# Second layer of a graph network kernel: node rows kept as two halves in F32R, one 320-column product per node tile, and one tile of each edge group fetched by TensorE

## The reference

```python
h = jnp.maximum(_layernorm(x, axis=-1), 0.0)
ss, vv = (s[src], v[src])                      # rows of h by source node
dot = jnp.einsum('eui,ei->eu', vv, e1)
out0 = C0 * (ss * e0 @ W1 + dot * INV3 @ W2)
...                                            # out1: three more products of ss, vv, e0, e1
m_agg = jax.ops.segment_sum(m, dst, num_segments=n)
...                                            # hs, hv = m_agg @ Ws, Wv
return x + jax.nn.relu(h)
```

## Time and profile before

| what | value |
|---|---|
| runs | 1919.09, 1921.43, 1923.35 us |
| profiled execution, span (the page gives no other time of it) | 1922.0 us |
| PE busy | 1773.5 us, 92% |
| POOL busy | 1405.2 us, 73% |
| DVE busy | 1376.6 us, 72% |
| ACT busy | 179.3 us, 9% |
| second layer, first to last gather | 1023.07 to 1904.05 us |

### The profile page before, as it was taken

The page is one execution under the profiler, slowest core; times in us unless marked ns, Lnnn a source line. Parts: engine busy times, 40 slices in busy tenths (PEclk is TensorE's granted clock), DMA queues, the critical chain, the costliest instruction groups (busy, mean ns, idle before and its releaser), DMA issues.

```text
span 1922.0 us, 59005 instructions
## 1 busy us (share of the span) xinstructions
PE 1773.5 (92%) x16922; PEld 1554.1 (81%) x16922; DVE 1376.6 (72%) x2841; ACT 179.3 (9%) x415; POOL 1405.2 (73%) x1498
## 2 busy tenths in 40 slices
PE   8989898989999988889875999999999999999998
PEld 6567676767667676767645899999999999999998
DVE  7888887878787878878878466656656565666654
ACT  5100000010010100000032000000000000000000
POOL 4677777777777777777755777777777777777774
PEclk9999999999999999999987999999999999999999
DMA  7433344333343333333323323223222323223323
GB/s 251 122 103 106 104 105 106 105 105 106 95 114 94 105 105 104 106 105 105 103 77 97 76 73 78 76 72 77 73 76 73 76 72 76 76 73 76 75 74 92
DMA packets 113339, 181.97 MB, mean 95 GB/s; under 512 B 31272, under 2 KB 80720, under 8 KB 112848
## 3 DMA queue, kind: packets, MB, share of 16 engines
q0 software_dynamic: 70272, 120.03, 25.2%
q1 hardware_dynamic: 35592, 55.14, 9.1%
q10 hardware_dynamic: 7112, 2.94, 0.6%
HBM read 170.94 MB, written 7.05 MB: 93 GB/s over the span
## 4 chain that ended last, share of the span: by engine, by line
POOL 43%; PE 26%; issue 18%; ACTq 6%; DVE 4%; DMA 1%; ACT 1%; POOLq 0%; DVEq 0%
POOL g L841 42%; PE sums L1147 8%; PE sums L1132 5%; PE w_ps L1100 5%; ACTq L733 5%; PE hid_ps L1086 3%; PE sums L1157 2%; DVE work L997 1%; ACT work L867 1%; DMA g<-node_table 1%; ACTq L730 1%; DVE work L991 1%; PE w_ps L604 1%; PE sums L576 0%; ACT lin_sb L873 0%
## 5 line engine op out<-in xcount | busy, mean ns | idle before, releaser
L841 POOL DMA_INDIRECT g<-node_table,src x1453 | 1379.4, 949 | 468.4 <-issue 439.1
L1147 PE MATMUL w_ps<-H,work 128*128 128x160 f32 x2900 | 404.3, 299 | 1.5 <-issue 1.5
L1147 PEld LDWEIGHTS w_ps<-H,work 128*128 128x128 f32 x2900 | 398.0, 190 | 1.7 <-issue 1.7
L997 DVE TENSOR_TENSOR work<-w_ps,g 128x384 f32<-128x384 f32 (+3 forms) x693 | 297.4, 456 | 54.0 <-PE w_ps L1100 33.0
L1016 DVE STREAM_TRANSPOSE turned<-sums 128x160 f32<-128x160 f32 x232 | 79.5, 342 | 322.6 <-PE sums L1157 224.5
L1100 PE MATMUL w_ps<-fc_sb,work 64*128 64x224 f32 x1612 | 219.1, 378 | 96.3 <-ACT work L867 59.4
L1132 PEld LDWEIGHTS sums<-work,sel 128*32 128x32 f32 x6448 | 198.5, 111 | 111.1 <-issue 68.2
L1100 PEld LDWEIGHTS w_ps<-fc_sb,work 64*128 64x128 f32 x1612 | 169.5, 191 | 130.6 <-DVE work L991 82.6
L945 DVE TENSOR_TENSOR sel<-mixed,sh 128x896 f32<-128x896 f32 x232 | 251.6, 1084 | 27.6 <-DVE mixed L941 2.1
L1132 PE MATMUL sums<-work,sel 128*32 128x160 f32 x6448 | 246.9, 304 | 1.9 <-DVE work L991 1.0
L1136 PE MATMUL sums<-g,sel 128*128 128x160 f32 x1612 | 238.2, 301 | 9.8 <-DMA g<-node_table,src 9.8
(11 more groups left out here) (103 smaller groups left out, 709.5 us busy)
## 6 DMA issues: line engine op xcount, KB each, us to landing
g<-node_table SPq DMA_DIRECT2D x2304, 0.6 KB
g<-node_table ACTq DMA_DIRECT2D x2304, 0.6 KB
feat<-edge_feat_dram SPq DMA_DIRECT2D x60, 512.0 KB
g<-node_table,src POOLq DMA_INDIRECT x1453
named<-src_rows_dram SPq DMA_DIRECT2D x30, 192.0 KB
X<-x_dram SPq DMA_DIRECT2D x5, 400.0 KB, 6.6
named<-src_rows_dram SPq DMA_DIRECT2D x30, 64.0 KB
sh<-edge_sh_dram SPq DMA_DIRECT2D x1, 1624.0 KB, 9.0
```

What stands on the lines that cost most here:

```text
L841: nc.gpsimd.indirect_dma_start(out=g[:, slot(p, u, j), :], out_offset=None, in_=table[layer], in_offset=bass.IndirectOffsetOnAxis(ap=src[: ...
L997: nc.vector.tensor_tensor(blocks(at), w[:, :, 2 * S_CH + j * V_CH:2 * S_CH + (j + 1) * V_CH].unsqueeze(2).to_broadcast([P, n, m, V_CH]), r ...
L1147: last = nc.tensor.matmul(found_at[:, i, 0:D], match[layer][i][:, t, :], H[:, t, :], start=(t == 0), stop=(t == NT - 1))
```

## The change

Only the second layer and what lies before it change (beside a regrouping of the first layer's code that leaves its instructions as they were).

- `split` holds for each node tile 320 columns in F32R: the upper half (ACT copies `H` with its conversion) and the remainder (VectorE subtracts that from `H`). One `find` is now 25 products of F32R operands with 320 columns.
- TensorE fetches one tile of every group (`PICKS`: tile 6 of groups 0, 1, 2 of a turn, tile 5 of group 3), 115 in all, and GpSimd issues no gather for these.
- ACT casts the indices for a whole turn in two pieces: `cast_early` for three tiles into PSUM (`hid_ps`), `cast_late` for the fourth into SBUF (`late_named`). VectorE's casts go.
- VectorE adds the two 160-column halves from PSUM into `g` (`join`, a TENSOR_REDUCE over two) in the place of ACT's copy.
- VectorE's order in a stage is now select, turn, compare for the group after the next, join for the next group. Match tiles: groups 1 and 3 of a turn share one; one lies over `H`, so the layer's compares wait until the table's DMAs have read `H`.

```diff
-PICKED = ((2,), (0, 2))
-MORE_AT = ((), (0,1,2))
+PICKS = ((0, 6), (1, 6), (2, 6), (3, 5))
+MATCH_OF = (0, 1, 2, 1)
+BANK_OF = (0, 1, 2, 3)
...
+        split = nc.alloc_sbuf_tensor_at("split", [P, NT, 2 * D], F32R, offset=arena_at)
+        match = [nc.alloc_sbuf_tensor_at(f"match{b}", [P, NT, P], F32R, offset=at)
+                 for b, at in enumerate((arena_at + 4 * SPLIT, arena_at + 4 * (SPLIT + NPAD), H_at))]
...
+        early_named = hid_ps[:, 0:EARLY * P].rearrange("p (i e) -> p i e", e=P)
+        late_named = arena_part(SPLIT + 2 * NPAD, P)
+        wanted_of = [early_named[:, i, :] for i in range(EARLY)] + [late_named]
...
+                        others |= {j for v, j in PICKS if v == u}
...
+                def cast_early(f, nxt):
+                    act.wait_ge(named_in[layer], 16 * f + (16 * nxt + 16))
+                    if nxt:
+                        act.wait_ge(match_done, NP * f + EARLY)
+                    nc.scalar.activation(early_named, named[:, 0:EARLY, :], ACT.Copy).then_inc(named_cast, 1)
+                def cast_late(f, nxt):
+                    if nxt:
+                        act.wait_ge(match_done, NP * f + NP)
+                    nc.scalar.activation(late_named, named[:, EARLY, :], ACT.Copy).then_inc(late_cast, 1)
...
+                def compare(f, i, nxt, s):
...
+                    dve.wait_ge(named_cast if i < EARLY else late_cast, f + (nxt + 1))
+...
                    nc.vector.tensor_tensor(match[MATCH_OF[i]][:], wanted_of[i].unsqueeze(1).to_broadcast(wide),
+                                            node_id_sb[:].unsqueeze(2).to_broadcast(wide),
+                                            ALU.is_equal).then_inc(match_done, 1)
+                def join(f, p, i, nxt, s):
+                    dve.wait_ge(found, NP * f + (NP * nxt + i + 1))
+                    nc.vector.tensor_reduce(g[:, slot(p, u, j), :], banks[:, BANK_OF[i], 0:2 * D].rearrange("p (h c) -> p c h", h=2),
+                                            AXX, ALU.add).then_inc(found_copied, 1)
...
-                        last = nc.tensor.matmul(found_at[:, i, 0:D], match[layer][i][:, t, :], H[:, t, :],
+                        last = nc.tensor.matmul(banks[:, BANK_OF[i], 0:2 * D], match[MATCH_OF[i]][:, t, :], split[:, t, :],
...
+            act.wait_ge(h1_ready, BY_ACT)
+            nc.scalar.activation(split[:, 0:BY_ACT, 0:D], H[:, 0:BY_ACT, :], ACT.Copy).then_inc(upper_ready, 1)
+            act.wait_ge(h1_by_dve, len(by_dve))
+            nc.scalar.activation(split[:, BY_ACT:, 0:D], H[:, BY_ACT:, :], ACT.Copy).then_inc(upper_ready, 1)
...
+            for h, at in enumerate((slice(0, BY_ACT), slice(BY_ACT, NT))):
+                dve.wait_ge(upper_ready, h + 1)
+                last = nc.vector.tensor_tensor(split[:, at, D:2 * D], H[:, at, :], split[:, at, 0:D].bitcast(F32), ALU.subtract)
...
+            dve.wait_ge(rows1_out, 16 * len(pieces))
```

More of the change, by code:

```diff
@@ L28 @@
 I32 = mybir.dt.int32
+F32R = mybir.dt.float32r
 ALU = mybir.AluOpType
@@ L640, in edge_layer, with picks_at, exists, fetched @@
             pass_of = {}
[L641 to L658, removed]
-                u, nxt = (o + ahead) % UNROLL, (o + ahead) // UNROLL
[L661 to L670, removed]
+            def picks_at(o, s, ahead):
+                u, nxt = (o + ahead) % UNROLL, (o + ahead) // UNROLL
+                if s is not None and s + ahead >= GROUPS:
+                    return []
+                return [(i, nxt) for i in range(NP) if PICKS[i][0] == u]
+            def exists(i, s):
+                return s is None or s < GROUPS and PICKS[i][1] < tiles_of(s)
+            def fetched(s):
+                return s is None or UNROLL <= s < GROUPS - UNROLL
+            found_at = sums[:, 0, 256:256 + D]
             def tiles_of(s):
@@ L834, in gather @@
                     p = (it - LEAD) % PERIOD if it >= LEAD else -1
[L835 to L844, removed]
+                    group = UNROLL * it + u
+                    n = tiles_of(group)
+                    others = {TILES - 1} if by_row_at(p, u, TILES - 1) else set()
+                    if own_weights:
+                        others |= {TILES - 1} if u == PICKED0 and fetched(group) else set()
+                    else:
+                        others |= {j for v, j in PICKS if v == u}
+                    for h, (a, b) in enumerate(CHUNKS):
+                        own = [j for j in range(max(a, skip), min(b, n)) if j not in others]
+                        for j in own:
+                            missing = b - max(a, skip) - len(own) if j == own[-1] else 0
+                            nc.gpsimd.indirect_dma_start(
+                                out=g[:, slot(p, u, j), :], out_offset=None, in_=table[layer],
+                                in_offset=bass.IndirectOffsetOnAxis(ap=src[:, TILES * group + j:TILES * group + j + 1], axis=0),
+                            ).then_inc(gathered[u][h], 16 + 16 * missing)
                 with passes(pool) as r:
@@ L948, in select, with match_rows @@
                                             ALU.mult).then_inc(sel_done, 1)
[L950 to L961, removed]
+                def match_rows(f):
+                    dve.wait_ge(named_in[layer], 16 * f + 32)
+                    dve.wait_ge(match_done, f + 1)
+                    nc.vector.tensor_copy(wanted, named[:, 0, :]).then_inc(named_read, 1)
+                    dve.wait_ge(named_read, f + 2)
+                    dve.wait_ge(found, f + 1)
@@ L1039, in stage @@
                         else:
-                            compare(f, p, e, PICKED[layer][0], 0, 0, True)
-                    if s is None or s < GROUPS:
-                        select(f, it, o, s)
-                        if pick_after(o, s, p, 2):
-                            compare(f, p, e, (o + 2) % UNROLL, *pick_after(o, s, p, 2), s is not None and s + 2 < UNROLL)
+                            for u in range(2):
+                                for i, nxt in picks_at(0, s, u):
+                                    compare(f, i, nxt, s + u)
+                    live = s is None or s < GROUPS
+                    before = None if s is None else s - 1
+                    if live:
+                        select(f, it, o, s)
+                    if not own_weights:
+                        if s is None or 1 <= s <= GROUPS:
+                            turn(f, o - 1, before)
+                        if s == 0:
+                            for i, nxt in picks_at(o, s, 0):
+                                join(f, p, i, nxt, s)
+                        for i, nxt in picks_at(o, s, 2) if live else []:
+                            compare(f, i, nxt, None if s is None else s + 2)
+                        for i, nxt in picks_at(o, s, 1) if live else []:
+                            join(f, p, i, nxt, None if s is None else s + 1)
+                    if live:
                         if s == GROUPS - 2:
@@ L1056, in stage @@
                                 else:
-                                    compare(f, p, e, 2, 0, 1, False)
-                    if s is None or 1 <= s <= GROUPS:
-                        turn(f, o - 1, None if s is None else s - 1)
+                                    match_rows(f)
+                    if own_weights and (s is None or 1 <= s <= GROUPS):
+                        turn(f, o - 1, before)
                     if s == GROUPS:
```

142 lines of the change are left out of this document (98 added, 44 removed).

## The result

The changed kernel takes 1955.4 us (median of 4 runs, 1953.0 to 1957.7) and the kernel before 1920.3 beside it: a ratio of 1.018 with an interval of 1.0166 to 1.0193, so 1.8% slower. The prediction said 1956 us. The profiled execution has a span of 1955.8 us.

The account below looks back on a forecast made before the run. GpSimd's back-to-back gathers were taken as the bound, TensorE within 1% of it: span 1922.0 - 37.6 (30 gathers) + 70 (28 holds) + 2 (between layers) = 1956.4, so 1956 us; own range 1942 to 1982, taken as 1925 to 1984.

Parts of the forecast that it names:

- TensorE's part: Second layer's finds: 0.139 us a product, 3.5 us a find, PE busy 69.9 us a period in place of 90.8.
- GpSimd as the clock: Second layer: GpSimd's gathers run back to back at 1.2538 us a step and stay the bound, 95.3 us a period.
- 30 gathers: Second layer: TensorE makes 115 tiles, not 85, so 703 gathers become 673, taking 37.6 us off the path.
- The hold: Second layer: 28 fourth-group compares with two SBUF inputs each hold a gather 2.5 us, 70 us in all, bounds 58 to 93.
- The phase argument behind 2.5: Compares start 0.2 to 0.5 us into a gather step, next gather 0.75 to 1.0 later, hence holds of 2.4 to 2.6.
- VectorE: Second layer: more compares, fewer casts and twelve reduces a period make 70.2 us busy, 76 with accumulates' issue; not the bound.
- The reduce: VectorE's join in the second layer: 320 inputs at 0.49 us each, twelve a period, 5.9 us.
- Between the layers: Two VectorE subtracts with two SBUF inputs hold the second layer's first gathers, costing 2 us, bounds 0 and 4.5.
- only roughly: Gather at 1023.07, started under L1286: the hold rule expected 0.41 us more, 0.64 was measured.
- No hold: Rival: the compare from two SBUF inputs runs beside gathers without holding them, 1886 us; chance 0.10.
- TensorE the bound: Rival: products at 0.278 us put PE at 111.6 us a period, 2116 us; a lower clock does the same; chance 0.05.

Follow-up runs that it names:

- e1: Changed kernel, but VectorE first copies the fourth group's indices from SBUF into PSUM and compares from there; 1885.6 us, ratio 0.981 to the kernel before.
- e3: As e1, but TensorE fetches no tile for each turn's fourth group, 87 tiles in place of 115; 1919.7 us, ratio 1.000 to the kernel before.
- e2: Changed kernel with a second compare of each turn, for its second group, also reading both inputs from SBUF; 2029.5 us in a single run.
- e6: Changed kernel, but the fourth compare takes its node numbers from PSUM, its wanted indices still from SBUF; 1884.8 us, ratio 0.980 to the kernel before.
- e4: Kernel before, second layer's first compare each turn taking indices from SBUF; 2986.5 and 3039.6 us beside 3028 and 3070 of the kernel before, on another chip.

## Why the prediction was right

The forecast was 1956 us and the measurement 1955.4. The terms agree as well as the sum, with two exceptions below: the moment at which the compares start, and TensorE's part.

- **GpSimd as the clock.** It held: waits for others in the loop were 0.9 us in the changed kernel, and e1, e3, the change and e2 all follow its steps and holds to within 3 us.
- **30 gathers.** Right in number. They gave 39.9 us and not 37.6, since a step also became 1.2504 us from 1.2538. What shortened it isn't known: e1, e2 and e3 have the short step too, e6 1.2533, and with one profile of each it may belong to the execution and not to the kernel.
- **The hold.** The mechanism was right, and so was its size: 70.4 us measured against 70, 2.51 each against 2.5. The phase argument behind 2.5 is right only on average. The compares did not lock at 0.2 to 0.5 us into a step. In 17 of 28 turns the held gather came 0.94 to 1.21 us after the compare's start and lost 2.14 to 2.38; in eight it came 0.00 to 0.17 after and lost 3.15 to 3.32. In the remaining three a gather started up to 0.02 us ahead of the compare and passed, and the next one was held for 2.14. The start that the prediction worked out, 0.75 to 1.0 us ahead of the next gather, was met in 2 turns of 28. So the bounds of 2.08 and 3.33 were derived and held, but that the two kinds average 2.5 is luck.
- **TensorE.** The find was taken at 3.5 us and takes 3.93; the product was mis-sized, 0.157 us for 0.139. PE is busy 77.9 us of the stretch where 69.9 were forecast: the finds are busy 47.0 for the 41.7 of the forecast, and the aggregates, ahead of which PE now waits for gathers (17.4 us), are busy 28.4 for 24.6. Nothing hung on it, since a product would have had to take 0.22 us before TensorE became the bound.
- **VectorE.** The reduce was forecast at 0.49 us and takes 0.483. Busy 69.0 us in the period, forecast 70.2.
- **Between the layers.** 1.7 us against 2. What I had not seen: the first compare started 7.7 us late, behind ACT's first cast, which itself stood behind five copies for which ACT waited. GpSimd was a turn ahead, so it cost nothing. The layer's first gather, which the prediction fitted "only roughly", ends 1.06 us behind L1361 (L1286 before) in both kernels, where every other gather longer than 1.1 us in that layer ends 0.82 behind; the 0.24 are open.
- **The rivals.** "No hold" gave 1886 us as its time; e1 removes the hold and takes 1885.6. "TensorE the bound" was not met: PE idled 17 of the 95.3 us.

The rule of the Trainium skill that two SBUF inputs contend with a GpSimd instruction that reads SBUF ("SBUF — State Buffer", "Who interferes with whom") agrees with e1, e6 and e2. The same section's inference that `tensor_tensor` leaves GpSimd's DMAs alone does not fit an indirect gather: it lost up to 3.32 us.

## What to carry to other kernels

Where GpSimd issues indirect DMAs back to back, look at each long VectorE instruction beside it and count its SBUF inputs. One input moved to PSUM, even by a copy of 0.27 us, gave back 2.5 us of gather for each. An engine that is 73% busy by the profile can be the bound if the rest of its time is "issue". And relief for an engine that is equal with another is worth only what the other loses as well: F32R took 3.0 us off each find of 6.96, and e3 gained nothing by it.

## What the runs showed of the hardware that I had not expected

- Whichever comes first holds up the other, but not for equally long. A gather that started 0.01 us into a compare took 4.26 us; one that started 0.04 us ahead took 0.95. In that second case it is the compare that pays. In 7 of 28 turns of the changed kernel a gather started 0.005 to 0.054 us ahead. With 0.054, 0.040, 0.019 and 0.005 us the compare took 3.470, 3.482, 3.504 and 3.520 us, as if it could read only from some 0.075 us after the gather's start (an estimate from these four). Twenty of the other compares took 3.45 and one 3.49. In e6, with one input in PSUM, compares that start 0.019 to 0.031 us behind a gather take 3.45 and the gathers 0.95.

```profile
1166.48 3.52 DVE L996 TENSOR_TENSOR match<-arena,node_id_sb 128x3200 fp32r<-128x3200 f32 x1
...
1166.48 0.94 POOL L848 DMA_INDIRECT g<-node_table,src  x1 [0.30 <-issue]
1167.74 3.08 POOL L848 DMA_INDIRECT g<-node_table,src  x1 [0.32 <-issue]
```

- The recorded order of the two starts decides only down to some 0.05 us. In e4 a gather recorded 0.04 us *into* the compare still passed, and the compare took 3.57 us in place of 3.49.

```profile
2139.15 3.57 DVE L965 TENSOR_TENSOR work<-wanted_sb,node_id_sb 128x3200 f32<-128x3200 f32 x1
...
2139.19 0.94 POOL L842 DMA_INDIRECT g<-node_table,src  x1 [0.30 <-issue]
2140.44 3.10 POOL L842 DMA_INDIRECT g<-node_table,src  x1 [0.30 <-issue]
```

- The granted clock was 0.90 in e3 from 1500 to 1900 us, with PE busy 319 of 400 us, and 1.00 in the kernel before with 90.8 of 91.5. e3's time was still that of its gathers.
- The F32R product's floor near 0.12 us below 256 columns, and that it lengthens at the low clock, above.
